# Adding two key tiles on POOL before the softmax sums: a cross-attention step with two tiled runs on PE in place of three

## The chip, the core and the metric

The kernel runs on one core of a Trainium2 chip. The metric is the device time of one execution in microseconds (us).

## What is computed

A gated block of a Flamingo model: cross attention of 16 batches of 100 queries on 361 keys, then a gated feed-forward layer with quantised weights. All is float32 at the interface. Cut to the attention, which the change touches:

```
b = 16, q_len = 100, kv_len = 361, d = 512, G = 4, Hpg = 4, dh = 32
Q = (layernorm(x) @ Wq).reshape(b, q_len, G, Hpg, dh) / sqrt(dh)
K = (ctx @ Wk).reshape(b, kv_len, G, dh);  V = (ctx @ Wv).reshape(b, kv_len, G, dh)
scores = einsum('bqghd,bkgd->bghqk', Q, K) + m * (k_index - q_index)
scores = where(mask, scores, neg)
w = softmax(scores, axis=-1)
out = einsum('bghqk,bkgd->bqghd', w, V).reshape(b, q_len, 512) @ Wo
x = x + tanh(g_xattn) * out
x = x + tanh(g_ffn) * down(rms_norm(silu(gate(ln(x))) * up(ln(x))))      (weights rounded to -1, 0, 1)
```

## The kernel before

Everything is written by hand, one instruction stream per engine (PE is the matrix engine, DVE, ACT and POOL work on tiles, SP issues transfers), ordered by semaphores. Three stages follow each other: projections of queries, keys and values (to 157 us), attention (to 367 us), and the feed-forward layer (to the end). While attention runs, POOL also quantises the feed-forward weights in 24 chunks of 128x1024.

Attention goes batch by batch. For a batch b PE makes two kinds of scores. The first kind, `scores` (L1161), has queries on partitions: 8 units u of two heads each, one unit in each half of `wide`. DVE takes the largest of each row (`row_max`, L894), negates it and splits it in two parts (`split_max`, L915 and L917). PE turns the maxima (`turn_maxima`, L1194), ACT copies them (`turned_max`, nm_t, recorded at L553), and SP stores them as two more rows of qs. The second kind, `scores_t` (L1175), has keys on partitions, 12 units j, four groups g for each of three key tiles kt of 120 or 121 keys; unit j uses bank j % 2. Since the maxima are rows of its operands, its result needs an exponential alone: ACT writes P to `p_t[:, j, :]` (`exps`, L644). P is held once, not twice.

`values_and_sums(b, kt)` then makes two products of a key tile's P. The first is with the values (L1185, into bank 2), the second with a block of ones (L1188, into bank 3), which gives the softmax's sums. Each product has four matmuls on four column tiles of 32 (`tile_position=(0, 32 * g)`) that run side by side; every matmul is float32 and shows as two instructions in the trace. The four column-tiled products of values and the four of ones are one *run*, and there are three runs for a batch. After the third, ACT copies both banks out (`keep_pv`, L657 and L658), takes log and exponential to get 1/sum (L665, L670), and DVE refines and applies it (`normalise`, steps 0 to 2, L924, L927, L932).

A *step* b of the loop on PE goes through units u = 0..7 of `scores(b, u)` and, behind each, the entries of a table `BEHIND[u]`, which work on older batches: ("t", 2, 4) is scores_t of unit 4 for batch b - 2, ("pv", 2, 0) the run of key tile 0 of batch b - 2, "turn" the turn of the maxima of b - 1. Two waits of PE matter below. `scores(b, u)` waits for the reduction of the unit two before it (L1161's wait on s_maxed), and `scores(b, 1)` also waits until ACT has copied the maxima of b - 1 (nm_ready), because the turn uses its bank. ACT's order inside a step is: exps 4 and 5 of b - 2, log and inverse of b - 3, nm_t of b - 1, exps 6 to 11 of b - 2, exps 0 to 2 of b - 1, `keep_pv(b - 2)`, exp 3 of b - 1. DVE's order is its 8 reductions with normalise steps 0 and 1 of batch b - 3 behind unit 3 and step 2 behind unit 5, then `split_max`. POOL's order before is the 24 chunks of `quantise` (L480, L482, L487, then the next load's issue L475), one after the other; the third operation of a chunk waits for the keys of a batch to be loaded.

## Time and profile before

| | |
|---|---|
| median of 3 runs | 578.21 us (577.47 to 579.21) |
| the profiled execution, its own time | 578.13 us |
| its span in the trace | 576.3 us (mean granted clock 0.956) |
| PE busy over the span | 501.7 us, 87% |
| DVE, ACT, POOL busy | 366.6, 346.5, 219.9 us |
| PE in the chain that ended last | 61% of the span |
| L1185, products with values | 384 instructions, 42.9 us busy |
| L1188, products with ones | 384 instructions, 41.7 us busy |

Busy time counts an instruction from its recorded start to its end. On PE these overlap, and the ends are modelled, so a busy PE can still have room; the distance from one start to the next says more. The step's length is read from the one instruction that comes once in a step, the turn of the maxima.

### The profile page before, as it was taken

How to read it: one execution, taken by the hardware profiler on the slowest of the kernel's cores; microseconds unless marked ns; L12 is line 12 of the kernel's file. 1: busy time of each engine (PE TensorE's matmuls, PEld its weight loads, DVE VectorE, ACT ScalarE, POOL GpSimd, SP SyncE). 2: the span in 40 equal slices, each digit the busy share in tenths (PEclk: the TensorE clock that was granted, in tenths of full speed). 3: DMA queues.
4: the chain of work that ended last, by engine and by line, in shares of the span. 5: the costliest groups of instructions: out<-in, count | busy, mean ns of one | idle time of the engine just before them, and what ended most of it. 6: DMA issues, size and time to landing. Idle time of an engine off the chain costs nothing.

```text
span 576.3 us, 8789 instructions
## 1 busy us (share of the span) xinstructions
PE 501.7 (87%) x3086; PEld 318.7 (55%) x3106; DVE 366.6 (64%) x671; ACT 346.5 (60%) x578; POOL 219.9 (38%) x238
## 2 busy tenths in 40 slices
PE   2699599979829989999999998589999999999984
PEld 1699599969815444444454444235555555555442
DVE  3785355336635778887788875266667666666751
ACT  1335658654204676666676676447777777777762
POOL 1010000000616532656364730155555556666540
PEclk9999989989956999999999999889999999999997
DMA  7778979999474675769777802000011111111000
GB/s 185 248 228 290 362 256 339 288 293 249 150 171 143 147 175 124 157 156 211 146 158 152 197 4 92 1 0 15 24 38 36 36 36 36 36 38 38 28 19 27
DMA packets 29259, 76.81 MB, mean 133 GB/s; under 512 B 4350, under 2 KB 15822, under 8 KB 27302
## 3 DMA queue, kind: packets, MB, share of 16 engines
q1 hardware_dynamic: 24038, 51.16, 33.7%
q0 software_dynamic: 3456, 12.58, 7.8%
q10 hardware_dynamic: 1728, 12.58, 6.5%
q8 instruction: 22, 0.36, 0.3%
q14 instruction: 15, 0.12, 0.1%
HBM read 57.29 MB, written 9.85 MB: 116 GB/s over the span
## 4 chain that ended last, share of the span: by engine, by line
PE 61%; DVE 11%; ACT 10%; issue 7%; DMA 6%; POOL 3%; SPq 1%; ACTq 0%; POOLq 0%; DVEq 0%
PE bank L1092 11%; PE wide L1255 9%; PE wide L1092 7%; PE bank L1185 6%; PE bank L1175 6%; PE wide L1161 6%; PE bank L1133 6%; PE bank L1188 5%; PE bank L1275 3%; DVE row_max L894 3%; DMA ct<-ctx_t 3%; ACT p_t L644 3%; ACT yq L760 2%; DMA wq_f<-wq 2%; DMA qs<-nm_t 1%
## 5 line engine op out<-in xcount | busy, mean ns | idle before, releaser
L894 DVE TENSOR_REDUCE row_max<-wide 100x2 f32<-100x722 f32 x128 | 110.3, 902 | 43.8 <-PE wide L1161 43.4
L644 ACT ACTIVATE p_t<-bank 121x400 f32<-121x400 f32 x192 | 92.6, 504 | 61.9 <-PE bank L1175 58.2
L1255 PE MATMUL wide<-w_q,xq 128*128 128x512 bf16 (+1 forms) x400 | 95.8, 384 | 1.8 <-ACT xq L691 0.8
L516 POOL TENSOR_TENSOR z<-h,lnw 128x512 f32<-128x512 f32 (+1 forms) x52 | 66.7, 1283 | 30.4 <-DVE h L1005 30.0
L1255 PEld LDWEIGHTS wide<-w_q,xq 128*128 128x128 bf16 (+1 forms) x416 | 39.5, 100 | 48.9 <-issue 6.4
L735 ACT ACTIVATE act<-wide,small 128x512 f32<-128x512 f32 (+1 forms) x52 | 35.7, 688 | 50.6 <-PE wide L1255 39.9
L1175 PE MATMUL bank<-qs,ks 103*121 103x400 f32 x144 | 51.4, 390 | 12.4 <-DMA qs<-nm_t 9.6
L1161 PE MATMUL wide<-ks,qs 101*100 101x362 f32 x192 | 51.8, 357 | 9.4 <-DVE row_max L894 8.3
L487 POOL TENSOR_SCALAR w_q<-quant_in 128x1024 bf16<-128x1024 f32 x24 | 29.3, 1223 | 74.9 <-DMA ks<-m_scratch 45.5
L1275 PE MATMUL bank<-w_q,yq 128*128 128x512 bf16 (+1 forms) x204 | 50.5, 392 | 2.3 <-ACT yq L760 1.0
L475 POOL DMA_DIRECT2D quant_in<-w_ffn x24 | 14.3, 596 | 98.9 <-DVE small L885 92.4
L867 DVE TENSOR_TENSOR ctl<-ct,cth 128x1445 fp32r<-128x1445 f32 x16 | 27.4, 1720 | 35.3 <-ACT cth L553 35.3
L1133 PE MATMUL bank<-wv_f,ct 128*121 128x128 f32 x384 | 47.4, 283 | 2.8 <-DMA ct<-ctx_t 2.8
L1133 PEld LDWEIGHTS bank<-wv_f,ct 128*121 128x121 f32 x384 | 46.7, 194 | 3.1 <-DMA ct<-ctx_t 3.1
L1005 DVE TENSOR_TENSOR h<-act,wide 128x512 f32<-128x512 f32 (+1 forms) x52 | 35.3, 681 | 17.7 <-ACT act L735 17.3
L1161 PEld LDWEIGHTS wide<-ks,qs 101*100 101x100 f32 x192 | 29.4, 174 | 31.0 <-issue 17.4
L1185 PE MATMUL bank<-p_t,v_all 120*32 120x400 f32 (+1 forms) x384 | 42.9, 519 | 0.0
L1188 PE MATMUL bank<-p_t,ones_keys 120*32 120x400 f32 (+1 forms) x384 | 41.7, 507 | 0.0
L1175 PEld LDWEIGHTS bank<-qs,ks 103*121 103x121 f32 x144 | 26.0, 190 | 25.6 <-ACT p_t L644 11.1
L1011 DVE TENSOR_REDUCE small<-z 128x1 f32<-128x1024 f32 (+1 forms) x26 | 31.6, 1214 | 13.5 <-POOL z L516 13.5
L480 POOL TENSOR_SCALAR quant_in<-quant_in,small 128x1024 f32<-128x1024 f32 x24 | 28.7, 1196 | 13.1 <-DMA quant_in<-w_ffn 12.2
L1275 PEld LDWEIGHTS bank<-w_q,yq 128*128 128x128 bf16 (+1 forms) x208 | 19.7, 102 | 24.2 <-issue 3.6
(137 smaller groups left out, 945.7 us busy)
## 6 DMA issues: line engine op xcount, KB each, us to landing
quant_in<-w_ffn POOLq DMA_DIRECT2D x24, 512.0 KB, 6.4
ct<-ctx_t SPq DMA_DIRECT2D x16, 722.0 KB, 8.4
abs_b<-w_ffn ACTq DMA_DIRECT2D x8, 1024.0 KB, 7.6
ks<-k_all SPq DMA_DIRECT2D x36, 181.0 KB
q_scratch<-qhl SPq DMA_DIRECT2D x16, 400.0 KB, 4.8
qs<-q_scratch SPq DMA_DIRECT2D x12, 400.0 KB
abs_a<-w_ffn ACTq DMA_DIRECT2D x4, 1024.0 KB, 7.6
xb<-x SPq DMA_DIRECT2D x12, 256.0 KB, 2.6
```

Of the source, the lines that this page charges most:

```text
L516: nc.gpsimd.tensor_tensor(z[par][0:rows, c], h[0:rows, c], lnw[0:rows, c], ALU.mult).then_inc(z_done, 1)
L644: nc.scalar.activation(p_t[:, j, :], bank[j % 2][0:KT, 0:HQ], ACT.Exp).then_inc(exp_done, 1)
L735: nc.scalar.activation(silu_g[j % 2][0:rows, :], wide[j % 2][0:rows, 0, :], ACT.Silu, scale=f_cg[par][0:rows]).then_inc(silu_done, 1)
L894: nc.vector.tensor_reduce(row_max[b % 2][:, 2 * u:2 * u + 2], wide[u % 2][0:SQ, :, 0:SK], AX_X, ALU.max).then_inc(s_maxed, 1)
L1092: mm = nc.tensor.matmul(dst, a, b, start=(n == 0), stop=(n == last))
L1133: mm = nc.tensor.matmul(bank[2 + b % 2][0:KT, kt * P:(kt + 1) * P], tile[:, c * SK + k0:c * SK + k0 + KT], wv_f[:, c, :], start=(c == 0), ...
L1161: mm = nc.tensor.matmul(wide[u % 2][0:SQ, k, 0:SKP], qs[b % SLOTS][0:ROWS_S, g, h * SQ:(h + 1) * SQ], ks[b % SLOTS][0:ROWS_S, g, :], start ...
L1175: nc.tensor.matmul(bank[j % 2][0:KT, 0:HQ], ks[b % SLOTS][:, g, KT_AT[kt]:KT_AT[kt] + KT], qs[b % SLOTS][:, g, :], start=True, stop=True). ...
L1185: nc.tensor.matmul(bank[2][32 * g:32 * g + 32, 0:HQ], v_all[0:n, b, kt * P + DH * g:kt * P + DH * (g + 1)], p_t[0:n, kt * G + g, :], start ...
L1188: mm = nc.tensor.matmul(bank[3][32 * g:32 * g + 32, 0:HQ], ones_keys[0:n, :], p_t[0:n, kt * G + g, :], start=(kt == 0), stop=(kt == 2), ti ...
L1255: mm = nc.tensor.matmul(wide[j % 2][0:rows, m, :], xq[:, c, 0:rows], w_q[:, m * C + c, 512 * j:512 * j + 512], start=(c == 0), stop=(c == ...
L1275: mm = nc.tensor.matmul(bank[1][0:rows, :], yq[:, k, 0:rows], w_q[:, 2 * C + k // 4, (k % 4) * D:(k % 4 + 1) * D], start=(k == 0), stop=(k ...
```

## The change

From batch 4 on (`PAIR_FROM`), POOL adds the P of key tiles 0 and 1 into a third tile `p_pair` (121x1600, `add_pair`). The product with ones then runs over two blocks, `p_pair` and key tile 2, in place of three. The product with values stays as it was. PE takes a second table, `BEHIND_PAIR`, from step 6 on: one run holds the values of tiles 0 and 1, the other the values of tile 2, the ones on `p_pair` ("a") and the ones on tile 2 ("s"). The semaphore pv_done is split into pv_value and sum_done, pair_added is new, and ACT waits for them before it writes over P. POOL's chunks of quantisation are dealt out to the steps, with `add_pair(b - 2)` behind those of step b, and the last two additions stand around `ln_rstd(0)`. `oh` and `ol` get room of their own; `p_pair` takes their old place.

```diff
+PAIR_FROM = 4
+BEHIND_PAIR = {0: [("t", 2, 4), ("t", 2, 5), ("t", 2, 6), ("turn", 1, 0), ("t", 2, 7)],
...
+               3: [("t", 2, 10), ("v", 2, 0), ("v", 2, 1)],
+               4: [("t", 2, 11), ("t", 1, 0)],
+               5: [("t", 1, 1)],
+               6: [("t", 1, 2), ("v", 2, 2), ("a", 2, 0), ("s", 2, 2)],
+               7: [("t", 1, 3)]}
...
+            def add_pair(b):
+
+                if b == PAIR_FROM:
+                    pool.wait_ge(wo_low, 1)
+                else:
+                    pool.wait_ge(sum_done, sums_before(b - 1) + 1)
+                pool.wait_ge(exp_done, b * UNITS + 2 * G)
+                nc.gpsimd.tensor_tensor(p_pair[:, :, :], p_t[:, 0:G, :], p_t[:, G:2 * G, :], ALU.add).then_inc(pair_added, 1)
+
             load_quant(0)
             load_quant(1)
-            for n in range(QN):
+            n = 0
+            for b in range(1, B):
+                while n < QN and n < 2 * b and stored_under(n) <= b:
+                    quantise(n)
+                    n += 1
+                if b >= PAIR_FROM + 2:
+                    add_pair(b - 2)
+            for n in range(n, QN):
                 quantise(n)
...
             o_low(0)
+            add_pair(B - 2)
             ln_rstd(0)
+            add_pair(B - 1)
             o_low(1)
...
                     if j % G == 0 and b > 0:
-                        act.wait_ge(pv_done, b * 3 - (2 - j // G))
+                        act.wait_ge(pv_value, b * 3 - (2 - j // G))
+                        if j == 2 * G:
+                            act.wait_ge(sum_done, sums_before(b))
+                        elif b > PAIR_FROM:
+                            act.wait_ge(pair_added, b - PAIR_FROM)
+                        else:
+                            act.wait_ge(sum_done, sums_before(b - 1) + j // G + 1)
...
+            def pair_sums(b):
+
+                n = KT_USED[0]
+                pe.wait_ge(pair_added, b - PAIR_FROM + 1)
+                for g in range(G):
+                    mm = nc.tensor.matmul(bank[3][32 * g:32 * g + 32, 0:HQ], ones_keys[0:n, :], p_pair[0:n, g, :],
+                                          start=True, stop=False, tile_position=(0, 32 * g))
+                mm.then_inc(sum_done, 1)
...
-            scores_t(B - 1, 4)
-            scores_t(B - 1, 5)
-            values_and_sums(B - 1, 0)
-            scores_t(B - 1, 6)
-            scores_t(B - 1, 7)
+            for j in (4, 5, 6, 7):
+                scores_t(B - 1, j)
             turn_xq(0)
             scores_t(B - 1, 8)
             scores_t(B - 1, 9)
-            values_and_sums(B - 1, 1)
+            values(B - 1, 0)
+            values(B - 1, 1)
             gate_up(0, (0,))
             scores_t(B - 1, 10)
             scores_t(B - 1, 11)
             gate_up(0, (1,))
-            values_and_sums(B - 1, 2)
+            values(B - 1, 2)
+            pair_sums(B - 1)
+            sums(B - 1, 2)
```

How the order on the engines moves, in step b = 11 as an example. In these rows `wide<-ks,qs` is a half of a score unit (x2 is one unit), `bank<-qs,ks` is scores_t, and a product with P is counted by its four column tiles. First PE at the start of the step, before:

```order
L1161 MATMUL wide<-ks_74,qs_71 100x362 x2
L1175 MATMUL bank<-qs_70,ks_73 121x400 x2
L1185 MATMUL bank<-p_t,v_all 32x400 x4
L1188 MATMUL bank<-p_t,ones_keys 32x400 x4
L1194 MATMUL wide<-ident,nm_q 32x100
L1175 MATMUL bank<-qs_70,ks_73 121x400 x2
L1161 MATMUL wide<-ks_74,qs_71 100x362 x2
```

and in the changed kernel:

```order
L1206 MATMUL wide<-ks_74,qs_71 100x362 x2
L1220 MATMUL bank<-qs_70,ks_73 121x400 x3
L1253 MATMUL wide<-ident,nm_q 32x100
L1220 MATMUL bank<-qs_70,ks_73 121x400
L1206 MATMUL wide<-ks_74,qs_71 100x362 x4
```

The run of key tile 0 that stood between the first two score units is gone from there; three units of scores_t, the turn and a fourth unit stand in its place.

PE in the second half of the step, from unit 4 to the next step's first unit, before:

```order
L1161 MATMUL wide<-ks_74,qs_71 100x362 x2
L1175 MATMUL bank<-qs_late,ks_late 121x400
L1161 MATMUL wide<-ks_74,qs_71 100x362 x2
L1175 MATMUL bank<-qs_late,ks_late 121x400 x2
L1185 MATMUL bank<-p_t,v_all 32x400 x4
L1188 MATMUL bank<-p_t,ones_keys 32x400 x4
L1161 MATMUL wide<-ks_74,qs_71 100x362 x2
L1175 MATMUL bank<-qs_late,ks_late 121x400
L1161 MATMUL wide<-ks_74,qs_71 100x362 x2
L1161 MATMUL wide<-ks_72,qs_69 100x362 x2
```

and in the changed kernel, from scores_t of unit 11 behind score unit 4 to the last unit of scores_t:

```order
L1220 MATMUL bank<-qs_70,ks_73 121x400
L1220 MATMUL bank<-qs_late,ks_late 121x400
L1206 MATMUL wide<-ks_74,qs_71 100x362 x2
L1220 MATMUL bank<-qs_late,ks_late 121x400
L1206 MATMUL wide<-ks_74,qs_71 100x362 x2
L1220 MATMUL bank<-qs_late,ks_late 121x400
L1230 MATMUL bank<-p_t,v_all 32x400 x4
L1247 MATMUL bank<-p_pair,ones_keys 32x400 x4
L1238 MATMUL bank<-p_t,ones_keys 32x400 x4
L1206 MATMUL wide<-ks_74,qs_71 100x362 x2
L1220 MATMUL bank<-qs_late,ks_late 121x400
```

The run behind unit 5 has moved behind unit 6 and has three blocks of four in it, so it now stands between score units 6 and 7.

POOL around the chunk that is quantised in the same step, before:

```order
L480 TENSOR_SCALAR quant_in_66<-quant_in_66,small 128x1024 [waits quant_loaded1]
L482 TENSOR_SCALAR quant_in_66<-quant_in_66 128x1024 [waits quant_step]
L487 TENSOR_SCALAR w_q<-quant_in_66 128x1024 [waits qk_in3,quant_step]
L475 DMA quant_in_66<-w_ffn 128x1024 [waits quant_done]
L480 TENSOR_SCALAR quant_in_65<-quant_in_65,small 128x1024 [waits quant_loaded0]
```

and in the changed kernel:

```order
L500 TENSOR_SCALAR quant_in_66<-quant_in_66,small 128x1024 [waits quant_loaded1]
L502 TENSOR_SCALAR quant_in_66<-quant_in_66 128x1024 [waits quant_step]
L507 TENSOR_SCALAR w_q<-quant_in_66 128x1024 [waits qk_in3,quant_step]
L495 DMA quant_in_66<-w_ffn 128x1024 [waits quant_done]
L519 TENSOR_TENSOR p_pair<-p_t 121x1600 [waits exp_done,sum_done]
L500 TENSOR_SCALAR quant_in_65<-quant_in_65,small 128x1024 [waits quant_loaded0]
```

Between the issue of a load and the next chunk's first operation stands the addition, which waits for P of the first two tiles.

## Rows read from the trace of the kernel before

**Rows 1.** Stretch us, its length; busy us (instructions) PE, PEld, DVE, ACT, POOL; clock; DMA

```profile
229.00:334.00 105.00, 97.98 (x697) 49.66 (x693) 86.42 (x117) 70.29 (x155) 60.02 (x55) 1.00 0.74 162
```

**Rows 2.** PE in order of time: first and last turn of the steps concerned

```profile
229.18 0.26 PE L1194 MATMUL wide<-ident,nm_q 100*32 100x100 f32 x1
...
334.18 0.26 PE L1194 MATMUL wide<-ident,nm_q 100*32 100x100 f32 x1
```

**Rows 3.** Chain of waits, one step: start us, us, what

```profile
272.43 0.92 DVE row_max L894
273.35 0.14 issue
273.49 0.55 PE wide L1161 x2
...
276.49 0.54 PE wide L1161 x2
```

**Rows 4.** PE in order of time, the second half of that step and the next start

```profile
282.00 0.88 PE L1185 MATMUL bank<-p_t,v_all 121*32 121x400 f32 x8
282.70 0.85 PE L1188 MATMUL bank<-p_t,ones_keys 121*32 121x400 f32 x8
283.49 0.57 PE L1161 MATMUL wide<-ks_late,qs_late 101*100 101x362 f32 x2
283.89 0.34 PE L1175 MATMUL bank<-qs,ks 103*121 103x400 f32 x1
284.07 0.49 PE L1161 MATMUL wide<-ks_late,qs_late 101*100 101x362 f32 x2
285.15 0.55 PE L1161 MATMUL wide<-ks,qs 101*100 101x362 f32 x2 [0.58 <-DVE row_max L894]
285.54 0.53 PE L1175 MATMUL bank<-qs,ks 103*121 103x400 f32 x2
286.00 0.88 PE L1185 MATMUL bank<-p_t,v_all 120*32 120x400 f32 x8
```

**Rows 5.** ACT in order of time, same step

```profile
275.04 0.54 ACT L665 ACTIVATE log_sum<-sum_kept 128x400 f32<-128x400 f32 x1
275.61 0.54 ACT L670 ACTIVATE inv_sum<-log_sum 128x400 f32<-128x400 f32 x1
276.10 0.24 ACT L553 ACTIVATE nm_t<-wide 32x100 fp32r<-32x100 f32 x1
276.31 3.09 ACT L644 ACTIVATE p_t<-bank 121x400 f32<-121x400 f32 x6
```

**Rows 6.** DVE in order of time, same step

```profile
277.07 2.56 DVE L894 TENSOR_REDUCE row_max<-wide 100x2 f32<-100x722 f32 x3 [1.67 <-PE wide L1161]
279.54 0.57 DVE L924 TENSOR_TENSOR log_sum<-sum_kept,inv_sum 128x400 f32<-128x400 f32 x1
280.14 1.38 DVE L927 SCALAR_TENSOR_TENSOR log_sum<-log_sum,inv_sum 128x400 f32<-128x400 f32 x1
```

**Rows 7.** POOL in order of time, same step

```profile
279.45 1.65 POOL L480 TENSOR_SCALAR quant_in<-quant_in,small 128x1024 f32<-128x1024 f32 x1
```

**Rows 8.** All engines in order of time, another step: POOL and DVE

```profile
232.33 1.13 POOL L480 TENSOR_SCALAR quant_in<-quant_in,small 128x1024 f32<-128x1024 f32 x1
...
232.93 0.96 DVE L924 TENSOR_TENSOR log_sum<-sum_kept,inv_sum 128x400 f32<-128x400 f32 x1
```

**Rows 9.** POOL groups by shape: mean ns behind the busy us

```profile
L507 POOL TENSOR_TENSOR ol<-o_t,oh 128x512 fp32r<-128x512 f32 x12 | 15.3, 1271 | 19.7 <-ACT oh L553 19.7
...
L507 POOL TENSOR_TENSOR ol<-o_t,oh 128x256 fp32r<-128x256 f32 x1 | 0.7, 725 | 0.0
```

**Rows 10.** POOL in order of time, one quantisation from issue to issue

```profile
171.70 0.58 POOL L475 DMA_DIRECT2D quant_in<-w_ffn  x1 [0.30 <-POOL w_q L487]
...
176.01 0.59 POOL L475 DMA_DIRECT2D quant_in<-w_ffn  x1 [0.30 <-POOL w_q L487]
```

**Rows 11.** DMA issues: KB each, us to landing

```profile
quant_in<-w_ffn POOLq DMA_DIRECT2D x24, 512.0 KB, 6.4
```

42 lines of the change are left out of this document (31 added, 11 removed).

## The prediction

> **What bounds the kernel now.** I read the busy time by stretch first, then the step's length, the chain of waits inside one step, and then each engine in order of time. In the stretch of the steps that the change touches [rows 1] PE is busy 98.0 of 105 us at the full granted clock (1.00), DVE 86.4, ACT 70.3 and POOL 60.0. So PE looks like the bound, and DVE is not far behind. Nine turns of the maxima after the first one, the tenth starts: (334.18 - 229.18) / 9 = 11.67 us for a step [rows 2]. In the chain [rows 3] a reduction ends at 273.35 and the step's first score unit starts at 273.49; I count all times below from there, as +x. The second score unit starts at +3.0.
>
> How much of the 11.67 us does PE need? From starts [rows 4]: a block of values 0.70 us (282.00 to 282.70), a block of ones with the way back to the full array 0.79 (to 283.49), one unit of scores_t 0.18 (283.89 to 284.07), a score unit 0.40 behind a run (283.49 to 283.89). Two units of scores_t and the way into a run take 0.46 (285.54 to 286.00), so the way in is 0.46 - 0.36 = 0.10 and the way out 0.79 - 0.70 = 0.09. Three runs are 3 x (0.70 + 0.79 + 0.10) = 4.8, twelve units of scores_t 2.2, eight score units at most 3.2: 10.2 us at most. PE therefore waits some 1.5 us in a step, and one of these waits is seen: 0.58 us for a reduction before 285.15 [rows 4]. The step is a weave of PE, ACT and DVE in which each wait is covered by a run, and not a plain sum of PE's work.
>
> **What is taken from PE.** One block of ones, 0.70 us, and one of three runs with its way in and out, 0.19: 0.89 us in a step. Ten steps (6 to 15) and, in the tail, two batches' blocks make 9 to 10 us.
>
> The Trainium skill (TensorEngine Tiling (Array Packing), "Key Properties") says that a change of tiling mode drains the array. The trace agrees, with 0.10 us in and 0.09 out; by the page's rule alone fewer runs are a gain, and the sum has it in already.
>
> **The first 3 us of the step do not get shorter.** ACT takes log at 275.04, the inverse at 275.61, copies the maxima at 276.10 and ends at 276.34; PE's second unit starts 0.15 later [rows 3, 5]. Before, the run of tile 0 lay under that chain. In the new order it is gone from there, but exps 4 and 5, log, inverse and copy stand on ACT as before, so the second unit still starts at about +3.0 and PE idles some 1 us. The gain of 0.89 has to come later in the step.
>
> **The addition.** The trace has no POOL operation of 1600 elements. It has the same kind, float32 with two inputs, at 512 elements, 1.271 us, and at 256, 0.725 us [rows 9]: 0.546 / 256 = 2.13 ns an element and 0.18 us fixed, so 0.18 + 1600 x 0.00213 = 3.6 us. Bounds: above, 1271 / 512 x 1600 = 4.0 (no fixed part); below, POOL's one-input operation, 1.13 us for 1024 elements [rows 8], which makes 1.13 / 1024 x 1600 = 1.8. I take 3.6, since rows 9 are the same kind of operation. It can start when exp 7 has ended. The six exps from 276.31 take 3.09 us [rows 5], one each 0.51, so exp 7 ends at 277.33 = +3.85. The addition runs from +3.9 to +7.5.
>
> **What the addition does to DVE.** This is the term that decides. DVE reduces units 1 to 3 from 277.07 and reaches normalise at 279.54 = +6.05 [rows 6]. `normalise` reads two tiles from SBUF, and such DVE operations and POOL operations exclude each other in this trace. L924 took 0.96 us in place of 0.57 when it came 0.60 us after a POOL operation of 1.13 us had started [rows 8]: it ended at 233.89, so with its own 0.57 it began at 233.32, 0.14 before the POOL operation's recorded end (233.46). And in the step followed here POOL's L480 took 1.65 us in place of 1.13 behind L924, and L927 then took 1.38 in place of 0.57 [rows 6, 7]: each waited out the other's instruction. So L924, due at +6.05, waits until about +7.4, and ends at +8.0. POOL's next operation, a chunk of quantisation that stands ready right behind the addition, takes its turn between L924 and L927, as in rows 6 and 7: L927 takes 1.38 again and ends at +9.4, where it ended at +8.03 before. Only then can DVE reduce unit 4, to +10.3.
>
> The Trainium skill (SBUF — State Buffer, "SBUF: two separate sides") states this as a rule against the change: the port pair that VectorE and GpSimd share is an exclusive lock, held "for the whole instruction", not a split of bandwidth. The rows bear it out for POOL operations of 1.1 us only; no row shows one of 3.6. If the lock were shared within an instruction, the first rival below would hold.
>
> **The walk to the end of the step.** Score unit 6 waits for the reduction of unit 4: +10.3 + 0.14 [rows 3] = +10.45. Before, it started at 283.49 = +10.0, right behind a run that is no longer there. Behind it PE has scores_t 2 of the next batch (+10.85) and the three-block run: in by +11.1, 0.70 + 0.70 + 0.79 = 2.2, out at +13.3 [rows 4]. Then unit 7 (0.40), one unit of scores_t (0.18), and the next step begins at +13.9. DVE's reduction of unit 6 is done by about +12.9 and does not hold it. **A step takes 13.9 us, 2.25 more.** For the nine steps 6 to 14: +20.2 us.
>
> ACT has cover: its exps 0 to 2 of the next batch wait for the addition until +7.5, where they started at +7.6 before. SP's transfers move with the step, nothing is put on its queue. The new semaphores and places cost nothing, they add no instruction to a full engine.
>
> **Step 15 and the tail.** Three chunks (21, 22, 23) stand before the addition of batch 13. A chunk from issue to issue is 176.01 - 171.70 = 4.3 us [rows 10], plus about 0.9 where it waits for DVE; its load lands 6.4 us after the issue [rows 11]. Chunk 21 ends in step 14 at 7.5 + 5.1 = +12.6 and issues the load of chunk 23, which lands at 12.6 + 6.4 = 19.0, that is 5.1 into step 15. Chunk 23 then takes 3.3 + 0.9, the addition starts at 9.3 in place of 3.9 and ends at 12.9. ACT's exp 0, on which scores_t 2 and the run stand, follows it: run at 13.8, unit 7 at 16.0 in place of 13.3. Step 15 costs 2.25 + 2.7 = 4.9. At the very end the last run has three blocks in place of two, +0.7, under no cover, since copy, log, inverse and normalise of batch 15 follow it one by one. The tail's other runs are paid back by ACT waits. Sum: 20.2 + 4.9 + 0.7 = **+25.8 us**. Against the profiled execution's own 578.13 us (0.08 below the median of 578.21) this is 604 us.
>
> **Rivals.**
> *No long lock, but no gain.* If L924 starts at +6.05 whatever POOL does, unit 6 no longer waits for DVE. But in the new order unit 4 stands behind the run of values at +6.9 (units 1 to 3 of the scores bring PE to +5.4, two blocks 1.5), scores_t 11 and 0 at +7.3 and +7.5, scores_t 1 waits for exp 11 to +8.3, then unit 6 at +8.6, the run +9.15 to +11.3, next step +11.9. That is 0.23 more than now, 2 us over nine steps. Step 15's late addition (its load has landed at +6.4 there, the addition ends at 6.4 + 3.3 + 3.6 = +13.3, and unit 7 comes at 16.4 in place of 11.3, of which I count 5) and 0.7 at the end add some 6: 586 us. A one-input price for the addition (1.8 us, ending at +5.7, before L924 is due) would give the same steps. For it: the long lock is not seen. Against it: every POOL and DVE pair that met waited for the whole of 1.1 us. Chance 0.12.
> *PE's work decides: faster.* POOL's 3.6 us fit in its idle time (60 of 105 us busy [rows 1], and 3.6 a step make 92 of 105), DVE's delay finds slack, and each step loses what PE loses, 0.89 us: 10 x 0.89 = 9, that is 569 us. It wins from the point at which L927 ends before about +7.3 and exp 5 to nm_t shrink by as much as PE does. For it: PE 93% busy. Against: +3.0 is ACT's chain, and DVE has no 1.4 us of slack before unit 6. Chance 0.07.
> *Lock, but half of it.* L924 waits for the addition, and POOL lets L927 through (quantisation not yet ready): 0.8 us less in a step, 13.1, hence 596 us. Or POOL falls behind in the steps with two chunks, and the addition starts later: two chunks 2 x 4.3 + 1.8 + 3.6 = 14.0, just a step, which gives up to 1 us more in half the steps, 610 us. Both are the forecast's mechanism with other sizes.
> *The change does nothing of what it says* is excluded: the order of the instructions shows two products with ones for a batch, and the addition between chunks.
>
> **How the numbers follow.** Forecast with its sizes (594 to 612) 0.78, no long lock 0.12, faster 0.07, no difference 0.03. Over 0.3%, 1.7 us, is what a measurement of this kernel can tell from no change; forecast and first rival both lie above it: slower 0.90, same 0.03, faster 0.07. The range that leaves out 2 in 10 at most is 586 to 612: from the first rival to the addition of 4.0 us (ten steps 0.4 longer, 608) with some of POOL's lag on top.
>
> **What would show it.** The turn of the maxima every 13.9 us in steps 6 to 14; an addition of 3.6 us on POOL from about +3.9; L924 at 1.8 to 2.0 us in place of 0.57 and L927 at about 1.4; score unit 6 and the long run waiting for row_max; PE busy falling from 93% to under 80% of the stretch. The second unit at +3.0 shows the ACT chain. Wrong would be: L924 at 0.57 while the addition runs (no long lock), steps under 11.5 us, or an addition that starts at +6 or later in most steps.

## The result, and the profile after

| | before | changed |
|---|---|---|
| median, runs side by side on one chip | 578.71 us (577.47 to 579.89, 4 runs) | 608.42 us (602.61 to 610.0, 4 runs) |
| the profiled execution, its own time | 578.13 us | 607.24 us |
| its span (mean granted clock) | 576.3 us (0.956) | 605.1 us (0.929) |
| turn of step 6, turn of step 16 | 229.18, 345.19 | 228.42, 370.16 |
| mean length of steps 6 to 14 | 11.67 us | 13.93 us |
| step 15 | 11.01 us | 16.36 us |
| turn 16 to the end of the span | 231.1 us | 234.9 us |

The changed kernel is slower: ratio 1.050, interval 1.045 to 1.055. The forecast was 604 us in a range of 586 to 612, with 0.90 for slower. The profiled executions are 29.1 us apart, and the table says where: -0.8 before turn 6, +20.4 in steps 6 to 14, +5.4 in step 15, +3.8 behind turn 16, +0.3 outside the span.

First the stretch of the steps in the changed kernel, then the tail (columns as in [rows 1]).

```profile
229.00:334.00 105.00, 88.42 (x515) 46.31 (x515) 81.08 (x97) 54.98 (x128) 77.77 (x50) 0.89 0.59 130
...
386.00:392.00 6.00, 6.00 (x28) 1.94 (x28) 0.00 (x0) 0.71 (x3) 3.09 (x1) 0.58 0.01 3
```

Two things differ from [rows 1]. POOL is busy 78 us instead of 60, as the additions ask. And the granted clock is 0.89 where it was 1.00. That was not forecast.

Now one step on POOL and DVE in order of time. Its first score unit starts at 282.82, so +x is the time less 282.82.

```profile
286.80 3.60 POOL L519 TENSOR_TENSOR p_pair<-p_t 121x1600 f32<-121x1600 f32 x1 [6.09 <-ACT p_t L688]
290.40 1.43 POOL L500 TENSOR_SCALAR quant_in<-quant_in,small 128x1024 f32<-128x1024 f32 x1
```

```profile
286.60 2.54 DVE L939 TENSOR_REDUCE row_max<-wide 100x2 f32<-100x722 f32 x3 [1.61 <-PE wide L1206]
289.06 1.78 DVE L969 TENSOR_TENSOR log_sum<-sum_kept,inv_sum 128x400 f32<-128x400 f32 x1
290.87 1.38 DVE L972 SCALAR_TENSOR_TENSOR log_sum<-log_sum,inv_sum 128x400 f32<-128x400 f32 x1
```

The addition takes 3.60 us from +3.98. The three reductions, which read `wide`, pass beside it: 2.54 us for three, where the kernel before had 2.56 [rows 6]. `normalise` does not: L969 takes 1.78 us in place of its 0.57 [rows 6] and ends at 290.84, 0.44 us after the addition. L972 waits for the chunk's first operation, as before. PE shows who pays:

```profile
286.02 0.87 PE L1206 MATMUL wide<-ks_late,qs_late 101*100 101x362 f32 x4 [0.78 <-ACT nm_t L591]
...
293.12 0.57 PE L1206 MATMUL wide<-ks_late,qs_late 101*100 101x362 f32 x2 [1.60 <-DVE row_max L939]
293.53 0.35 PE L1220 MATMUL bank<-qs,ks 103*121 103x400 f32 x1
293.81 0.88 PE L1230 MATMUL bank<-p_t,v_all 121*32 121x400 f32 x8
...
295.96 0.58 PE L1206 MATMUL wide<-ks_late,qs_late 101*100 101x362 f32 x2
296.38 0.35 PE L1220 MATMUL bank<-qs,ks 103*121 103x400 f32 x1
296.56 0.50 PE L1206 MATMUL wide<-ks,qs 101*100 101x362 f32 x2
```

Unit 6 starts at 293.12 (+10.30) after a wait of 1.60 us for DVE's reduction, the three-block run at +10.99, unit 7 at +13.14, the next step at +13.74.

This step ran at the full clock. The clock was at 0.50, half of the full one, only in five stretches of the nine steps: 230.5 to 237.4, 244.2 to 247.7, 257.8 to 261.3, 271.5 to 278.4 and 329.5 to 333.0 us. Counted from first unit to first unit, the four steps without such a stretch take 13.74 to 13.78 us, the three with a short one 13.70 to 13.72, and the two with a long one 14.08 and 14.50. (The distance from turn to turn scatters more, 13.19 to 14.33, since the turn itself comes 0.6 us late in some steps.) In the slow steps unit 6 waits less for DVE: not at all or 0.6 us in place of 1.6. So already in this trace the full-clock steps have the whole loss of 2.1 us, and a short fall of the clock adds nothing to it.

### The profile page after: what moved, and what is told of

Read it like the earlier page. It is cut to its first block, busy times and chain, and to the rows that moved or that the text cites. A ratio compares the mean times of both kernels' runs of the same rounds, so it can differ in the third digit from the quotient of the medians.

```text
span 605.1 us, 8642 instructions
## 1 busy us (share of the span) xinstructions
PE 513.0 (85%) x3010; PEld 323.8 (54%) x3010; DVE 380.7 (63%) x671; ACT 342.5 (57%) x578; POOL 267.1 (44%) x250
## 3 DMA queue, kind: packets, MB, share of 16 engines
q0 software_dynamic: 3456, 12.58, 7.3%
q10 hardware_dynamic: 1728, 12.58, 6.3%
## 4 chain that ended last, share of the span: by engine, by line
PE 54%; DVE 14%; ACT 12%; issue 8%; DMA 7%; POOL 2%; SPq 1%; ACTq 0%; POOLq 0%; DVEq 0%
PE wide L1321 10%; PE bank L1137 10%; PE wide L1137 7%; PE wide L1206 6%; PE bank L1230 5%; DVE row_max L939 5%; PE bank L1220 4%; DMA abs_b<-w_ffn 4%; PE bank L1178 3%; PE bank L1341 3%; PE bank L1238 3%; ACT p_t L688 2%; DVE log_sum L972 2%; ACT yq L805 2%; DVE log_sum L969 2%
## 5 line engine op out<-in xcount | busy, mean ns | idle before, releaser
L688 ACT ACTIVATE p_t<-bank 121x400 f32<-121x400 f32 x192 | 90.0, 502 | 85.9 <-PE bank L1220 81.7
L1321 PE MATMUL wide<-w_q,xq 128*128 128x512 bf16 (+1 forms) x416 | 99.4, 389 | 0.8 <-ACT xq L736 0.8
L1206 PE MATMUL wide<-ks,qs 101*100 101x362 f32 x192 | 54.9, 382 | 16.9 <-DVE row_max L939 10.8
L1220 PE MATMUL bank<-qs,ks 103*121 103x400 f32 x144 | 54.6, 412 | 15.4 <-DMA qs<-nm_t 10.2
L519 POOL TENSOR_TENSOR p_pair<-p_t 121x1600 f32<-121x1600 f32 x12 | 43.9, 3658 | 47.9 <-ACT p_t L688 47.8
L1230 PE MATMUL bank<-p_t,v_all 120*32 120x400 f32 (+1 forms) x384 | 48.2, 604 | 0.0
L507 POOL TENSOR_SCALAR w_q<-quant_in 128x1024 bf16<-128x1024 f32 x24 | 32.4, 1350 | 34.6 <-DMA ks_late<-m_scratch 19.8
L1178 PE MATMUL bank<-wv_f,ct 128*121 128x128 f32 x384 | 44.9, 274 | 0.0
L1220 PEld LDWEIGHTS bank<-qs,ks 103*121 103x121 f32 x144 | 28.6, 203 | 29.2 <-ACT p_t L688 16.1
L1056 DVE TENSOR_REDUCE small<-z 128x1 f32<-128x1024 f32 (+1 forms) x26 | 31.6, 1214 | 13.5 <-POOL z L552 13.5
L1137 PE MATMUL bank<-cth,wk_h 128*128 128x362 f32 x64 | 23.6, 369 | 12.5 <-DVE ctl L912 12.5
```

Of the source, the lines that this page charges most:

```text
L519: nc.gpsimd.tensor_tensor(p_pair[:, :, :], p_t[:, 0:G, :], p_t[:, G:2 * G, :], ALU.add).then_inc(pair_added, 1)
L688: nc.scalar.activation(p_t[:, j, :], bank[j % 2][0:KT, 0:HQ], ACT.Exp).then_inc(exp_done, 1)
L1137: mm = nc.tensor.matmul(dst, a, b, start=(n == 0), stop=(n == last))
L1178: mm = nc.tensor.matmul(bank[2 + b % 2][0:KT, kt * P:(kt + 1) * P], tile[:, c * SK + k0:c * SK + k0 + KT], wv_f[:, c, :], start=(c == 0), ...
L1206: mm = nc.tensor.matmul(wide[u % 2][0:SQ, k, 0:SKP], qs[b % SLOTS][0:ROWS_S, g, h * SQ:(h + 1) * SQ], ks[b % SLOTS][0:ROWS_S, g, :], start ...
L1220: nc.tensor.matmul(bank[j % 2][0:KT, 0:HQ], ks[b % SLOTS][:, g, KT_AT[kt]:KT_AT[kt] + KT], qs[b % SLOTS][:, g, :], start=True, stop=True). ...
```

## The experiments

Four theories run through them. A: the addition shuts DVE out, L969 and L972 are late, and unit 6 with them. B: PE's clock falls because the new table leaves PE without work at the start of a step. C: the addition's length on ACT's way from exp 7 to exp 0. D: POOL's queue, with two chunks in a step, brings the addition late. The expectations of the first four runs (tiny_add, norm_early, add_in_4, before_pool_add) do not mention the clock; B comes in with the runs after them. "Mean step" is that of steps 6 to 14, "clock" the granted clock of 229 to 334 us; a kernel with one run has no interval.

### Taking each suspect away

**tiny_add.** The addition covers 8 of 400 columns of each block. The softmax's sums then come from wrong data; the order of all instructions is unchanged.

```diff
+                    nc.gpsimd.memset(p_pair[:, :, :], 1.0).then_inc(pair_set, 1)
...
-                nc.gpsimd.tensor_tensor(p_pair[:, :, :], p_t[:, 0:G, :], p_t[:, G:2 * G, :], ALU.add).then_inc(pair_added, 1)
+                nc.gpsimd.tensor_tensor(p_pair[:, :, 0:8], p_t[:, 0:G, 0:8], p_t[:, G:2 * G, 0:8], ALU.add).then_inc(pair_added, 1)
```

> The changed kernel, but POOL adds 8 of the 400 columns of each group in place of all (the rest of the third tile holds ones from one fill at batch 4), so the sums are not the softmax's. All waits, the order on PE, ACT and DVE and the chunks of quantisation stay. Theory (DVE's normalise waits for the long addition): the wait of L924's counterpart falls from 1.2 us to that behind a quantisation operation, at most 1.1 and mostly under 0.5, a step falls from 13.9 to between 11.9 and 12.9 us, and the kernel takes 584 to 595 us. Rival (the new order on PE, with a three-block run between score units 6 and 7, costs the time itself): steps stay at 13.9, 605 to 608 us. Second rival (ACT's exps wait for the addition): the same fall as the theory, but with L924's counterpart not shorter.

Measured: 599.76 us (1 run), mean step 13.63 us, clock 0.81. The waits behind the addition are gone, and yet a step is only 0.3 us shorter. That lies between the two forecasts and fits neither. The clock is lower than in the changed kernel (0.81 against 0.89). Undoing A does not give the loss back.

**norm_early.** DVE does `normalise` steps 0 and 1 behind unit 0 of the step, before the addition starts.

```diff
+NORMALISE_EARLY = {0: (0, 1), 5: (2,)}
...
-                        for step in NORMALISE_BEHIND.get(u, ()):
+                        for step in (NORMALISE_EARLY if b >= PAIR_FROM + 2 else NORMALISE_BEHIND).get(u, ()):
```

> The changed kernel, with normalise steps 0 and 1 behind score unit 0 in place of unit 3 from step 6 on. There they come at about +2.7 from the step's start, when the inverse is ready, and end by +3.9, before the addition starts. Nothing else changes. Theory: L969 and L972 fall back to 0.57 us each, unit 4's reduction starts at about +7.5 in place of +9.4, a step takes 12.5 to 12.9 us, the kernel 594 to 598 us. Rival (the order or ACT's wait costs the time): about 607 us, steps of 13.9, though both operations are short.

Measured: 608.42 us (4 runs), ratio 1.054 (1.047 to 1.062), mean step 13.78 us, clock 0.87. A miss: the waits of DVE went, but the time stayed, as the rival had it. (The ratio goes by another measurement of the kernel before, 579.09 us, so it is not to be set beside the 1.050 of the changed kernel.) DVE, then the stretches around it, then PE in order of time:

```profile
284.40 0.57 DVE L970 TENSOR_TENSOR log_sum<-sum_kept,inv_sum 128x400 f32<-128x400 f32 x1 [0.78 <-ACT inv_sum L716]
285.01 0.58 DVE L973 SCALAR_TENSOR_TENSOR log_sum<-log_sum,inv_sum 128x400 f32<-128x400 f32 x1
```

```profile
286.00:288.00 2.00, 1.54 (x7) 0.84 (x11) 1.90 (x3) 0.98 (x3) 2.00 (x1) 0.65 0.10 16
288.00:290.00 2.00, 2.00 (x16) 0.39 (x8) 0.23 (x1) 0.16 (x1) 2.00 (x2) 0.50 0.00 0
```

```profile
287.55 2.75 PE L1231 MATMUL bank<-p_t,v_all 120*32 120x400 f32 x16
290.23 0.58 PE L1207 MATMUL wide<-ks_late,qs_late 101*100 101x362 f32 x2
```

The two blocks of values take 2.68 us from start to start; in the step of the changed kernel shown above, at the full clock, they took 1.48 (288.24 to 289.72). A granted clock of 0.50 is the 1.2 GHz level. Before it fell PE had waited 0.78 us for nm_t (ahead of 284.65) and 0.58 for a reduction (ahead of 286.46).

**after_filled, norm_filled, tiny_filled.** The three kernels again (changed, norm_early, tiny_add), with matmuls whose result nobody reads put into PE's waits: 5 behind unit 0 and 2 behind unit 2 (and 7 behind unit 5 in after_filled). They hold PE up a little themselves: unit 1 starts 0.24 us behind ACT's copy of the maxima in tiny_filled, 0.14 us in tiny_add, and in four of the nine steps of the other two 0.5 us behind it. Those steps are the ones whose turn comes late. The seven ahead of unit 6 in after_filled fit under the wait for DVE: in a step with them unit 6 starts 0.95 us behind the start of unit 4's reduction, as it does in the step of the changed kernel above.

```diff
+FILL = {0: 5, 2: 2, 5: 7}
...
+            def fill(n):
+
+                for _ in range(n):
+                    nc.tensor.matmul(bank[3][:, HQ:512], ident[:, :], ident[:, 0:512 - HQ], start=True, stop=True)
+
...
+                if PAIR_FROM + 2 <= b < B:
+                    fill(FILL.get(u, 0))
```

> The changed kernel, with matmuls that nobody uses (identity by identity into 112 free columns of bank 3, about 0.19 us each at full clock) in PE's waits of steps 6 to 15: five behind score unit 0, two behind unit 2, seven behind unit 5. Nothing else waits for them. In the changed kernel the granted clock of the steps' stretch fell to 0.89, before it was 1.00. Theory of two costs (DVE's wait for the addition, and the clock falling where PE waits): the clock of the stretch comes back to 0.98 or more, DVE's waits stay as they are, a step goes from 13.93 to 13.5 to 13.8 us and the kernel to 600 to 604 us. Rival (the clock's fall is a symptom without a price): 605 to 610 us with a clock of 1.00. Second rival (the idle of PE is all there is to it, and DVE's wait costs nothing): 592 us or less.

> The kernel with normalise steps 0 and 1 behind score unit 0, plus five unused matmuls behind unit 0 and two behind unit 2 on PE. Without them DVE's two operations no longer waited for the addition, but the granted clock fell once in each step, and the run of values took 2.68 us in place of 1.48. Theory: with the clock kept, steps of 12.5 to 12.8 us in place of 13.78, the kernel 594 to 598 us, clock of the stretch 0.98 or more. Rival (the clock is no cause; the new order's own waits are): steps stay near 13.8, 605 us or more.

> The changed kernel with the pair tile added in 8 of 400 columns (so the sums are not the softmax's) and with unused matmuls in TensorE's waits (5 behind unit 0, 2 behind unit 2): the new order of the runs without the long addition and without the fall of the clock. The addition alone, without the fills, gave steps 6 to 14 of 13.63 us at a granted clock of 0.81. If what tiny_add lost was the clock alone: granted clock 0.98 or more over 229 to 334 us, steps 11.9 to 12.3 us, kernel 582 to 590 us; the changed kernel's loss then divides into the addition's exclusion of VectorE and the clock. If the new order itself makes TensorE wait that long (probabilities of tile 2 late, unit 6 late): steps stay at 13 to 13.6 us at full clock, kernel 596 to 600 us.

Measured: after_filled 608.51 us (1 run), norm_filled 593.23 us (4 runs), ratio 1.021 (1.016 to 1.026), tiny_filled 593.26 us (1 run). By its time after_filled falls to its rival (605 to 610 us, the clock's fall has no price), by its steps it stands at the edge of its theory (13.5 to 13.8 us); its turn 6 comes 3.3 us later than in the changed kernel, in a part that the fills do not touch, so the steps are what to read. norm_filled's steps are as expected, its time 0.8 us under the range. tiny_filled, whose sums are wrong as in tiny_add, missed its forecast of 11.9 to 12.3 us and also the alternative (13 us and more).

The same stretch, for two of them:

after_filled:

```profile
229.00:334.00 105.00, 99.84 (x733) 67.23 (x732) 82.18 (x100) 56.73 (x132) 77.72 (x49) 1.00 0.65 138
```

norm_filled:

```profile
229.00:334.00 105.00, 98.00 (x703) 60.98 (x702) 79.29 (x109) 61.74 (x143) 84.66 (x57) 1.00 0.69 151
```

All three have the full clock (tiny_filled too, 1.00). The mean steps, by what is taken away:

| mean step, us (before: 11.67) | clock falls (granted clock of the stretch) | clock kept by fills |
|---|---|---|
| normalise waits for the addition | 13.93 (changed, 0.89) | 13.80 (after_filled) |
| normalise early | 13.78 (norm_early, 0.87) | 12.54 (norm_filled) |
| addition tiny | 13.63 (tiny_add, 0.81) | 12.58 (tiny_filled) |

**The two faults hide each other.** Take away one, and 0.13 to 0.30 us come back; take away both, and 1.4 us come back. While DVE holds unit 6, a slow stretch ahead of it lies under that wait; the changed kernel's own steps show that, as said above. While the clock is down, PE reaches unit 6 late by itself: in norm_early unit 6 waits for nobody, and the two blocks of values take 2.68 us. Taking one away also moves the other: the clock falls more where DVE's wait is gone (0.81 and 0.87 against 0.89).

Even with neither fault a step is 0.87 us (norm_filled) and 0.91 us (tiny_filled) over the 11.67 of before. In tiny_filled 0.1 us of it is the fills' own, and 0.3 us is quantisation still in the way (L976 takes 1.29 us in all nine steps, and unit 6 waits 0.3 for DVE). What the rest is was not shown. The new table has no run between its first four units, but putting the old table back did not return it: the ordinary steps of norm_three_runs below take 12.20 to 12.67 us.

### What the exclusion between POOL and DVE is

**add_in_4.** The addition as four instructions of 400 elements, back to back.

```diff
-                nc.gpsimd.tensor_tensor(p_pair[:, :, :], p_t[:, 0:G, :], p_t[:, G:2 * G, :], ALU.add).then_inc(pair_added, 1)
+                for g in range(G):
+                    add = nc.gpsimd.tensor_tensor(p_pair[:, g, :], p_t[:, g, :], p_t[:, G + g, :], ALU.add)
+                add.then_inc(pair_added, 1)
```

> The changed kernel, with the addition as four instructions of 400 elements (one a group) in place of one of 1600. By 0.18 + 400 x 0.00213 each takes 1.03 us, 4.1 us together. Theory of a lock held for one instruction: the wait of L969 falls from 1.2 us to at most 1.0, L972 then waits for the next piece (0.9) in place of a quantisation operation, the addition ends later; a step takes 13.4 to 13.8 us, the kernel 602 to 607 us. If the lock went by the whole of POOL's queue, L969 would wait 1.7 us, and the kernel would take 612 us or more. If POOL and DVE only slow each other, nothing changes but the 0.5 us longer addition: 608 to 612 us.

Measured: 620.89 us (1 run), mean step 15.60 us, clock 0.83. The steps run from 12.57 to 20.06 us. In four of the nine L971 takes 4.04 to 5.01 us. One of these, POOL and DVE:

```profile
247.36 4.00 POOL L520 TENSOR_TENSOR p_pair<-p_t 121x400 f32<-121x400 f32 x4
...
251.35 1.11 POOL L500 TENSOR_SCALAR quant_in<-quant_in,small 128x1024 f32<-128x1024 f32 x1
```

```profile
248.31 4.58 DVE L971 TENSOR_TENSOR log_sum<-sum_kept,inv_sum 128x400 f32<-128x400 f32 x1
```

Here DVE is not let in between two pieces. It waits for the rest of the four and also for the first operation of the next chunk, which follows without a gap. This is the second theory of the expectation, with a longer wait than it had (1.7 us). It does not hold in every step: in the other five L971 takes 0.56 to 0.57 us and is let in between the second piece and the third, which then takes 1.72 to 2.15 us in place of 1.02, though these follow each other without a gap too. In the four long cases L971 came 0.5 to 1.5 us after the addition's start, in the five short ones 2.3 to 2.7 us after it.

**add_in_4_wait.** The same with a semaphore wait of POOL on itself between the pieces.

```diff
+                    nc.gpsimd.tensor_tensor(p_pair[:, g, :], p_t[:, g, :], p_t[:, G + g, :], ALU.add).then_inc(piece_added if g < G - 1 else pair_added, 1)
+                    if g < G - 1:
+                        pool.wait_ge(piece_added, (b - PAIR_FROM) * (G - 1) + g + 1)
```

> The addition in four pieces of 400 elements as before, but POOL waits on a semaphore for each piece before it starts the next. In four pieces without a wait L969's counterpart waited 4.0 us and more, for all four. Theory (POOL gives the ports back only where it waits between instructions): now DVE gets in between two pieces, L969's counterpart takes at most 1.6 us in all, and the step is 13.3 to 13.9 us, the kernel 600 to 608 us. Rival (shorter pieces always make it worse, because a DVE operation that waits is served only when POOL's queue is empty): 615 us or more, as without the waits (620.9).

Measured: 605.61 us (1 run), mean step 14.30 us, clock 0.89. One step:

```profile
283.83 5.04 POOL L521 TENSOR_TENSOR p_pair<-p_t 121x400 f32<-121x400 f32 x4 [2.29 <-ACT p_t L692]
```

```profile
286.09 0.57 DVE L973 TENSOR_TENSOR log_sum<-sum_kept,inv_sum 128x400 f32<-128x400 f32 x1
286.69 1.29 DVE L976 SCALAR_TENSOR_TENSOR log_sum<-log_sum,inv_sum 128x400 f32<-128x400 f32 x1
```

L973 never takes more than 0.71 us now, and L976 waits for the rest of one piece. That holds also in the four steps of 6 to 14 in which it came early, 0.8 to 1.3 us after the addition's start, as in add_in_4's long cases. So for an early comer it is POOL's wait that opens the way. The addition takes 1 us longer, for the most part because its third and fourth piece wait for DVE in turn (1.50 and 1.25 us in place of 1.02). With the clock still falling the kernel gains little. The mean step missed its range of 13.3 to 13.9 us by two steps of 16.03 and 17.47, in which PE waits 2.2 us for an exponential of ACT, and ACT for the late addition (theories C and D).

**before_pool_add and before_pool_set.** The kernel before, with its three runs and its sums, plus an unused POOL operation of 121x1600 at the addition's place: once an addition of a tile of zeros to itself, once a fill that only writes. Both deal out the chunks as the change does.

```diff
+                pool.wait_ge(exp_done, b * UNITS + 2 * G)
+                nc.gpsimd.tensor_tensor(idle[:, :, :], idle[:, :, :], idle[:, :, :], ALU.add).then_inc(idle_done, 1)
```

> The kernel before, with its own order on PE and three runs, and with POOL's chunks dealt out as in the changed kernel and an addition of 121x1600 at the same place (from batch 4, behind exp 7), whose operands and result nobody else uses. No engine waits for it. Theory: L924 waits 1.2 us or more behind it, as in the changed kernel, unit 4 to 7 of the scores come late, a step takes 12.9 to 13.2 us in place of 11.67, and the kernel 590 to 596 us. Rival (POOL's work does not matter, the order does): 578 to 581 us.

> As the kernel before with an unused addition on POOL, but POOL's operation only writes its 121x1600 elements (a fill with zeros) and reads nothing. No row shows such an operation; by its size it takes 1.3 to 2.9 us. If a POOL operation that only writes also shuts out DVE's two-input operations, the late ones cost as with the addition: L924's counterpart takes up to 0.57 plus the fill, and the kernel takes 584 to 594 us. If it doesn't, L924's counterpart takes 0.57 us behind the fill, only quantisation's operations delay DVE, and the kernel takes 578 to 583 us.

Measured: before_pool_add 593.70 us (1 run), clock 0.93, four of the nine steps 11.66 to 11.68 us, five 12.01 to 15.99; before_pool_set 577.27 us (1 run), every step 11.64 to 11.68 us, clock 1.00. In a long step of the first, POOL, DVE and PE:

```profile
243.57 2.87 POOL L511 TENSOR_TENSOR idle<-idle 121x1600 f32<-121x1600 f32 x1
246.42 1.11 POOL L488 TENSOR_SCALAR quant_in<-quant_in,small 128x1024 f32<-128x1024 f32 x1
```

```profile
244.43 3.53 DVE L950 TENSOR_TENSOR log_sum<-sum_kept,inv_sum 128x400 f32<-128x400 f32 x1
```

```profile
250.16 0.57 PE L1187 MATMUL wide<-ks,qs 101*100 101x362 f32 x2 [1.73 <-DVE row_max L920]
```

and in the second kernel POOL and DVE at the same place:

```profile
242.38 1.45 POOL L509 MEMSET idle<- 121x1600 f32 x1
```

```profile
243.84 0.56 DVE L948 TENSOR_TENSOR log_sum<-sum_kept,inv_sum 128x400 f32<-128x400 f32 x1
```

The fill ended at 243.83, 0.01 us before DVE's operation was due, and in no step did the two meet. So this run says nothing on whether a POOL operation that only writes shuts DVE out. It is a control for the other: dealing the chunks out and a short operation at that place cost nothing. The addition in the old order costs 14.6 us (one run of 593.70 against a median of 579.09 for the kernel before on that chip) with PE's work unchanged. The time fell in its range, but not by the expected way, a loss in every step. Where the addition starts early (2.85 us from 230.58) L950 takes 1.11 us and the step is 11.67; where two chunks stand ahead of it, L950 comes soon behind its start, takes 3.44 to 3.53 us, PE waits, and in three of the four cases its clock falls. That is theory D, true in this kernel. In the changed kernel the addition starts at +3.97 to +3.98 in eight of the nine steps, and the step is long without D.

The Trainium skill (SBUF — State Buffer, "Who interferes with whom") has the shared port pair taken for one whole instruction. L969 in the changed kernel and the short case here agree:

```profile
232.76 1.11 DVE L950 TENSOR_TENSOR log_sum<-sum_kept,inv_sum 128x400 f32<-128x400 f32 x1
```

Both end 0.4 us behind the addition, though the chunk's first operation follows it without a gap. The long L950 does not agree: it ends at 247.96, 1.5 us behind the addition's end at 246.44, so it waited for L488 too. add_in_4's long cases show the pair held over up to four pieces and a fifth instruction. There the measurements decide. In steps 6 to 14 the undivided addition let DVE in at its end where DVE's operation came 2.2 to 2.9 us after its start (the changed kernel, after_filled, five steps here), and did not in the four where it came 0.9 us after it. But in step 15 of the changed kernel L972 came 0.8 us after the start and was let in. What decides is open.

### How far the idea can be mended

**norm_filled_q15.** norm_filled with the last step's two chunks behind its addition.

```diff
-                while n < QN and n < 2 * b and stored_under(n) <= b:
+                while n < (QN - 2 if b == B - 1 else QN) and n < 2 * b and stored_under(n) <= b:
...
-            for n in range(n, QN):
-                quantise(n)
...
             o_low(0)
+            for n in range(QN - 2, QN):
+                quantise(n)
             add_pair(B - 2)
```

> norm_filled with the last step's two last chunks (22 and 23) quantised behind the last pair addition instead of ahead of it. Theory: step 15's 16.46 us in norm_filled (11.01 before) is long because GpSimd takes three chunks ahead of its addition, so step 15 falls to 13 to 13.7 us and the kernel ends 2.5 to 3.5 us earlier than norm_filled, at about 590 us (1.015 to 1.017 of the kernel before). Rival: the chunks were only passed on, something else (the wait for the reductions, o_low) holds the last product with ones, step 15 stays above 15.5 us and the kernel stays at 593 us; or the time comes back after turn 16, as later quantised chunks hold the projection.

Measured: step 15 12.56 us in place of 16.46, more than expected (13 to 13.7); behind turn 16 the span has 235.1 us in place of 234.1. The kernel takes 591.9 us (5 runs), ratio 1.024 (1.020 to 1.028), where 1.015 to 1.017 was expected: against norm_filled's 1.021 the ratios do not show the 3 us that the steps do. The time before turn 6, which the edit doesn't touch, differs by 2.6 us between the two profiles (225.88 and 228.44), about as much.

**norm_three_runs.** norm_early with the table in the kernel before's order: values of tile 0 behind unit 0, of tile 1 behind unit 3, and only tile 2 with the two blocks of ones behind unit 5. Three runs in place of two, no fills.

```diff
+BEHIND_PAIR = {0: [("t", 2, 4), ("t", 2, 5), ("v", 2, 0), ("turn", 1, 0), ("t", 2, 6), ("t", 2, 7)],
...
+               3: [("t", 2, 11), ("v", 2, 1)],
...
+               5: [("t", 1, 1), ("t", 1, 2), ("v", 2, 2), ("a", 2, 0), ("s", 2, 2)],
```

> norm_early (normalising steps 0 and 1 ahead of the addition) with the kernel before's table of where the three tiles' runs stand: tile 0's product with values behind unit 0, tile 1's behind unit 3, only tile 2's with the two-block product with ones behind unit 5; no unused matmuls. It asks whether TensorE keeps its clock when useful work lies under the first 3 us of ScalarE's work instead of fills. Theory: with tile 0's run there, granted clock is 0.98 or more over 229 to 334 us, steps 6 to 14 12.4 to 12.9 us, kernel 591 to 597 us, against 13.78 us and 608 us of norm_early. Rival: the clock falls as in norm_early because the addition's wait alone leaves the gap: clock under 0.92, steps 13.5 us or more, kernel above 603 us.

Measured: 602.95 us (1 run), clock 0.95. It lies between the two forecasts, and for a plain reason: eight steps take 12.20 to 12.67 us, one 19.12. That one, DVE and PE:

```profile
243.46 5.55 DVE L973 SCALAR_TENSOR_TENSOR log_sum<-log_sum,inv_sum 128x400 f32<-128x400 f32 x1
```

```profile
249.88 0.93 PE L1207 MATMUL wide<-ks,qs 101*100 101x362 f32 x2 [5.44 <-DVE row_max L940]
```

An addition (3.57 us) and a chunk's first operation (1.12) ran back to back and shut L973 out for both; PE waited 5.44 us, and its clock stood at 0.50 from 244.8, early in that wait, to 255.1. A normal step of this kernel waits too, but in small pieces with a run between them, and keeps the full clock. Its last wait shown here is theory C:

```profile
286.65 0.55 PE L1207 MATMUL wide<-ks_late,qs_late 101*100 101x362 f32 x2 [0.65 <-ACT nm_t L592]
...
291.73 0.44 PE L1221 MATMUL bank<-qs,ks 103*121 103x400 f32 x1 [0.50 <-ACT p_t L689]
```

```profile
291.18 1.54 ACT L689 ACTIVATE p_t<-bank 121x400 f32<-121x400 f32 x3 [1.41 <-POOL p_pair L520]
```

Why L973 was caught in that one step is open. In three other steps it came as shortly ahead of an addition that followed POOL's work at once (0.45 to 0.47 us, against 0.45) and took 0.57 to 0.58 us.

The first of the two waits shown, 0.65 us for nm_t, was not there in the kernel before. There the block of ones of tile 0, 0.70 us, lay under ACT's work; without it PE stands still for nearly as long. With the 0.50 for ACT the new waits take more than the block gave.

**three_runs_guarded.** norm_three_runs, with POOL waiting for DVE's second normalising operation before an addition, and step 15's chunks behind.

```diff
+                if b < B - 2:
+                    pool.wait_ge(newton_step, 2 * b)
                 pool.wait_ge(exp_done, b * UNITS + 2 * G)
```

> norm_three_runs with two edits: GpSimd waits for VectorE's second normalising operation before it starts an addition (in norm_three_runs one of ten additions started 0.45 us after that operation had been issued, which then took 5.55 us, the addition and the chunk behind it; PE waited 5.44 us and its clock fell for that step of 19.12 us), and the last step's chunks 22 and 23 stand behind its addition, as in norm_filled_q15. No unused matmuls. Theory (VectorE held by back-to-back GpSimd work, and the clock falling only where TensorE's wait is long): no step over 12.8 us, mean of steps 6 to 14 12.3 to 12.5, step 15 12 to 13, granted clock 0.98 or more over 229 to 334 us, kernel 585 to 591 us, still 1.0 to 2.0 per cent over the kernel before. Rival: the long step came from something else (a late load, two chunks) and returns: mean 13 us or more, kernel above 595 us.

Measured: 591.44 us (4 runs), ratio 1.025 (1.015 to 1.034), mean step 12.71 us (12.38 to 13.16), step 15 12.29, clock 0.98. The long step is gone, as it should be if that collision was its cause. But it came in one step of nine and each kernel has one trace, so its absence is weak evidence by itself. The steps are a little longer than expected (a mean of 12.3 to 12.5, none over 12.8), and the kernel ends just outside its range. In the longest step, 13.16, the clock was at 0.50 from 306.8 to 310.2; in five of the others the addition starts 0.3 us later, behind its guard (2.37 us after the turn in place of 2.07), and PE's wait for ACT's exponential grows from 0.5 to as much as 0.79. The three mended kernels (ratios 1.021, 1.024, 1.025) do not differ beyond their intervals, and all three are slower than the kernel before.

## Why the prediction was right, point by point

**The walk through the step was right nearly throughout.** Forecast and measured, in the step shown: second unit +3.0 and +3.20; addition from +3.9 to +7.5 and from +3.98 to +7.58; L969 ends at +8.0 and at +8.02; L972 at +9.4 and +9.43; unit 6 at +10.45 and +10.30; run at +11.1 and +10.99; unit 7 at +13.3 and +13.14; next step at +13.9 and +13.74. The mean step is 13.93, and nine steps cost 20.4 us where 20.2 were forecast. That DVE's wait is the cause is borne out by the steps at the full clock (13.74 to 13.78) and by after_filled (13.80); taking DVE's wait away shortens the step only if the clock is kept as well (13.80 to 12.54). The size of the addition, 3.6 us from operations of 512 and 256 elements [rows 9], held: eleven of its 12 instances take 3.58 to 3.63 us, and the twelfth, 4.21, waited for L969 itself. One reading was too even: L969 takes 1.77 to 1.82 us in five steps, but 1.16 to 1.45 in the four with a slow stretch ahead of it, where DVE reaches it later; those steps are no shorter.

**What it left out: the clock.** The argument had PE idle for 1 us at the start and over 1 us before unit 6 and took the full clock for granted, since [rows 1] showed 1.00. The mean came out right because DVE's wait sets the end of the step and the slower PE mostly fits under it: only 0.13 us of a step is the clock's (13.93 against 13.80). That the number was spared the clock is luck, for the prediction did not weigh it. And the sentence that this term decides was too strong. Without the long exclusion the first rival had 11.9 us for a step and 586 us; tiny_add gave 13.63 us and 599.76. What the rival had wrong is the clock (1.05 us, 13.63 against 12.58) and 0.7 us more (12.58 against 11.9), of which 0.3 is unit 6 waiting for a DVE that quantisation holds and 0.1 the fills. The rival did not come true, but at its own condition it would have missed by 14 us.

**Step 15: the sum was right, its parts were not.** Forecast 4.9, measured 5.4 us. The addition was to start at +9.3, behind a load that lands late. It started at +6.4 (357.98, with the step's first unit at 351.57): the load of chunk 23 was issued at 350.58, as forecast 12.8 us into step 14, but landed 3.7 us later, at 354.30, where the prediction took the median of 6.4 [rows 11]. So chunk 23 was under way at +3.1. In exchange DVE's second operation was caught for longer than forecast, and the clock fell:

```profile
357.98 4.21 POOL L519 TENSOR_TENSOR p_pair<-p_t 121x1600 f32<-121x1600 f32 x1
```

```profile
358.76 3.86 DVE L972 SCALAR_TENSOR_TENSOR log_sum<-log_sum,inv_sum 128x400 f32<-128x400 f32 x1
```

```profile
357.56 2.87 PE L1230 MATMUL bank<-p_t,v_all 120*32 120x400 f32 x16
```

L972 waited out the whole addition, and PE ran its values at the lower clock, 2.79 us to the next start instead of 1.48. The failed step is the load that "lands at 12.6 + 6.4 = 19.0, that is 5.1 into step 15": it was in at +2.7. L972's wait (3.86 us where L927's price was 1.38) and the clock made up for it, which is luck. That the chunks ahead of the addition cost time is right: with them behind it, step 15 fell by 3.9 us.

**The tail was mis-sized: +0.7 forecast, +3.8 measured.** From the turn of step 16 to the end of the attention's last product it takes 21.6 us before (345.19 to 366.83) and 25.9 in the changed kernel (370.16 to 396.04, with 394.69 and 395.37 the starts of its last two blocks). The chain of waits of the changed kernel names the pieces:

```profile
384.58 0.61 PE wide L1310 x4
385.19 0.86 PE bank L1220 x2
386.05 2.83 PE bank L1230 x16
388.88 2.89 PE wide L1321 x8
...
395.37 0.67 PE bank L1238 x8
```

In the kernel before the same stretch, from PE's turn of xq at 358.71 to 366.83, is 8.1 us long with four blocks; here it is 11.5 with five. A block is 0.70, so 2.6 us are left, and they go with a clock of 0.58 from 386 to 392. (The kernel before has its clock at 0.50 only from 370.0, behind the last product.) The stretch ahead of the turn of xq is 0.9 us longer too, 14.4 against 13.5, with one block fewer; behind the last product 0.5 us come back. "The tail's other runs are paid back by ACT waits" is the step that failed: with the runs gone from under ACT, PE waits more and then runs slower. That the clock does it here is read from the trace; no run was made on the tail.

**The signs to look for.** Turns every 13.9 us on average, L969 at 1.8 (in five steps of nine) and L972 at 1.4 us (in all nine), the addition at +3.9, unit 6 waiting for row_max: all seen. "PE busy under 80% of the stretch" was wrong, it is 88.42 / 105 = 84%, because matmuls at the lower clock are recorded as busy for longer (2.87 us for sixteen against 1.55). From 284.4 to 325.7, at the full clock, PE is busy 77%, as forecast. The other rivals: "faster" needed ACT's chain to shrink and DVE to have slack, but unit 1 came at +3.20 and unit 6 waited 1.60 us for DVE. "Half of it" gives 596 or 610 us and so lies on both sides of the result, but neither of its reasons was seen: L972 waited in all nine steps, and the addition was not late in any.

## What to carry to other kernels

Work that moves from a full engine to an idle one is only free if the idle one shares nothing: ask for each instruction of 3 us what it shuts out and who stands in order behind that. Where PE is woven through waits of other engines, a run is also cover: count what each wait lies under after the change, and look at the granted clock by stretch. In these kernels PE lost in clock what it had gained in work. And if undoing the suspected fault gives nothing back, try it with a second suspect undone as well before you drop it; two faults that hide each other each look harmless alone.
